# A fused attention-like product and mixture layer on one core: the first stage's opening in pairs of row tiles, and the last product by halves

## The chip, the cores and the metric

The kernel runs as one program on one core of a Trainium2 chip. The metric is the device time of one execution in microseconds (us). A core has five engines with an instruction queue each: TensorE (PE in the profile, with its weight loads as PEld), VectorE (DVE), ScalarE (ACT), GpSimd (POOL) and SyncE (SP), which here only starts transfers. Each engine takes its instructions in the order in which they stand, and waits on semaphores where another engine has to be done first. Data lie in an on-chip memory of 128 partitions; matrix products land in PSUM, eight banks of 128x512 float32.

## The reference

```python
x = x + xattn(layernorm(x), ctx, s1, z1, s2, z2)     # x: (2, 1024, 2048), ctx: (2, 2048, 2048)
x = x + ffn(layernorm(x), W_base, b_base, W_router, lora_A, lora_B)

def fake_quant(x, s, z): q = clip(round(x / s + z), 0, 255); return (q - z) * s
def xattn(x1, x2, ...): return matmul(fake_quant(x1, s1, z1), fake_quant(x2, s2, z2))
def ffn(x, ...):                                       # 8 experts of rank 16, the best 2 of each token
    w = top-2 softmax weights of x @ W_router.T
    h = einsum('td,erd->ter', x, lora_A)
    return x @ W_base.T + b_base + 2.0 * einsum('ter,eor,te->to', h, lora_B, w)
```

So there are two large products for each of two batches of 1024 tokens: the quantised rows with the quantised context, 2048x2048, and then the normalised result with W_base, 2048x2048. The second is done in three float16 products (high and low parts) to keep its precision.

## The kernel before, in words

**First stage (0 to 303 us).** For each batch b the 1024 tokens are eight row tiles T of 128 tokens. A row tile of x is loaded (`load_rows`, 1 MB), VectorE takes its statistics in four `bn_stats` of 512 elements and a `bn_aggr` (`ln_stats_of`), ScalarE takes a root (`ln_std_of`), VectorE turns it into scale and shift by six operations on 128x1 (`ln_scale_of`), ScalarE writes the quantised bytes (`ln_bytes_of`, tile q1u), TensorE turns them in eight transposes (`turn`, into PSUM bank 6), and ScalarE copies them out as float16 (`ln_copy`, tile q1T). The context comes in 32 slices n of 128 output columns (16 for each batch), 1 MB each: `load_ctx`, then bytes on ScalarE (`ctx_bytes_of`), then float16 on VectorE (`ctx_ready_of`). The product of slice n is made in three chunks (n, c) of 342 token columns, 16 matmuls each (`chunk`): chunk 0 needs row tiles 0 to 2, chunk 1 tiles 0 to 5, chunk 2 all eight. The chunks go round four PSUM banks. VectorE takes each chunk out and adds x (`take_y`); after chunk 2 ScalarE adds a column (`col_add_of`), writes the high half for the second stage (`hi_of`) and squares (`sq_of`); VectorE writes the low half (`lo_of`) and sums the squares (`acc_of`).

The order is written out by hand, engine by engine. The first three slices are interleaved in a group, as `ORDER` (line 44) says; from slice 3 on a loop takes one slice after the other. The tiles of batch 1 are worked in between: tiles 8 and 9 in the opening, the others at the slices in `LN_AT`. The waits that matter here: `turn(T)` waits for the bytes of T and for the copy of T - 1, since all share bank 6; a chunk waits for its context slice, its row tiles, and for the take of the chunk four places ahead of it; `take_y` waits for xT's slice in memory too.

**The parameters.** s1, z1, s2, z2 are single numbers. Four transfers spread each of them to a column of 128 partitions (line 627). VectorE derives 21 more columns of `par` from them. SP waits for these four transfers behind the load of row tile 0, ahead of row tile 1.

**Second stage (303 to 345 us)** makes row sums, the router's logits and the low-rank parts. **Third stage (345 to 1027 us)** is the product with W_base. Batch 0 comes in 32 plain tiles of 128x512, 48 matmuls each. Batch 1 is done in eight units i of seven half-depth products p of 24 matmuls each (`multiply`), from which VectorE puts four output quarters q together by seven additions (`take`). A quarter's end (`out_of`) is five operations on 128x512: two that need no product (mean and shift, L1292 and L1294), then scale and add the low-rank part (L1296), times the row scale (L1298), plus bias (L1301). The low-rank part is three matmuls (`quarter_lora`) which ScalarE takes out (`lora_of`). Then SP stores the quarter, 256 KB.

## Time and profile before

| | us |
|---|---|
| median of 3 runs | 1029.69 (1028.73 to 1030.63) |
| the profiled execution | 1028.86 |
| its span, from the first to the last instruction recorded | 1027.1 |
| TensorE busy in the span | 967.9 (94%) |
| VectorE busy | 798.7 (78%) |
| ScalarE busy | 470.3 (46%) |
| granted TensorE clock, mean (1 is full) | 0.988 |

The profile's page gives sums and the chain of waits that ended last. The trace behind it is asked for windows (busy time of each engine in a stretch), for the timeline of an engine (equal neighbours merged) and for the transfers. Busy time of matmuls is not TensorE at its peak: a 342 column chunk takes longer when the granted clock is at its lower level.

### The profile page before, as it was taken

To read this page: it belongs to the slowest core of one execution; us is meant where nothing else is said; L and a number is where in the kernel's file an instruction comes from. 1 tells how busy PE (TensorE), PEld (TensorE's weight loads), DVE (VectorE), ACT (ScalarE), POOL (GpSimd) and SP (SyncE) were. 2 spreads that over 40 slices of the span, in tenths; PEclk is the share of its full clock that TensorE was granted. 3 is DMA by queue.
4 is the path that set the end of the run, shared out by engine and by line. 5 is a ranking of instruction groups with operands and counts; after the bars stand their busy time and mean duration, and the time that the engine had idled before them with its cause. 6 is when DMAs were issued, how large, how long until landed. Compare 5 with 4: busy or idle time off the path is not lost.

```text
span 1027.1 us, 15016 instructions
## 1 busy us (share of the span) xinstructions
PE 967.9 (94%) x5847; PEld 523.5 (51%) x5847; DVE 798.7 (78%) x1503; ACT 470.3 (46%) x492; POOL 18.7 (2%) x40
## 2 busy tenths in 40 slices
PE   0478999999999999999999999999999999999997
PEld 0355666666679844444444444444444444444443
DVE  6767899788763787896788687775788798798775
ACT  4769989688652245543454433312223223322300
POOL 0000000000000000000000000000000000000000
PEclk9989999999999999999999999999999999999999
DMA  7836777587734236886566665238643243233220
GB/s 301 338 119 226 256 277 291 205 292 302 274 129 138 91 132 186 238 263 206 184 204 180 182 236 196 67 103 291 221 149 113 78 149 112 78 134 102 83 72 31
DMA packets 62590, 185.64 MB, mean 181 GB/s; under 512 B 7432, under 2 KB 19768, under 8 KB 56248
## 3 DMA queue, kind: packets, MB, share of 16 engines
q1 hardware_dynamic: 58360, 174.18, 48.3%
q10 hardware_dynamic: 2880, 8.39, 2.1%
q0 software_dynamic: 1280, 2.12, 2.0%
q8 instruction: 46, 0.75, 0.3%
q14 instruction: 24, 0.20, 0.1%
HBM read 151.07 MB, written 33.60 MB: 180 GB/s over the span
## 4 chain that ended last, share of the span: by engine, by line
PE 74%; DVE 4%; DMA 2%; ACT 1%; issue 1%; DVEq 0%; ACTq 0%
PE pair L1638 30%; PE pair L1661 28%; PE pair L1501 10%; PE pair L1617 4%; DMA w_r<-in_w_n 1%; PE pair L1607 1%; DMA spread<-scratch 1%; DMA scratch<-w_max 1%; DVE w_p L1123 0%; ACT w_r L730 0%; ACT xt L665 0%; ACT ctx_u L659 0%; PE pair L1583 0%; PE pair L1516 0%; PE pair L1509 0%
## 5 line engine op out<-in xcount | busy, mean ns | idle before, releaser
L1638 PE MATMUL pair<-x2p,w_p 128*128 128x512 f16 x1536 | 336.7, 379 | 1.0 <-DVE w_p L1123 1.0
L1638 PEld LDWEIGHTS pair<-x2p,w_p 128*128 128x128 f16 x1536 | 150.2, 98 | 181.9 <-DVE w_p L1123 1.5
L1501 PE MATMUL pair<-q1T,ctx_q 128*128 128x342 f16 x1536 | 234.0, 314 | 4.7 <-DVE xt L926 4.7
L1501 PEld LDWEIGHTS pair<-q1T,ctx_q 128*128 128x128 f16 x1536 | 150.1, 99 | 83.2 <-issue 6.3
L1661 PE MATMUL pair<-x2p,w_slot 128*128 128x512 f16 x768 | 169.2, 379 | 0.0
L757 ACT ACTIVATE sq<-pair,lsc 128x512 f32<-128x512 f32 x64 | 43.6, 682 | 226.0 <-PE pair L1617 192.3
L1661 PEld LDWEIGHTS pair<-x2p,w_slot 128*128 128x128 f16 x768 | 75.1, 98 | 90.7
L785 ACT ACTIVATE w_slot<-w_q,usc 128x1024 f16<-128x1024 f32 x32 | 36.5, 1146 | 95.7 <-DVE usc L1331 27.2
L1661 PE MATMUL pair<-x2p,x2p 128*128 128x512 f16 x336 | 74.3, 379 | 0.0
L659 ACT ACTIVATE ctx_u<-ctx_f,par 128x2048 uint8<-128x2048 f32 x32 | 66.6, 2081 | 1.6 <-DVE ctx_q L911 1.4
L926 DVE SCALAR_TENSOR_TENSOR xt<-pair,par,xt 128x342 f32<-128x342 f32 (+1 forms) x96 | 54.4, 567 | 15.6 <-PE pair L1501 15.6
L785 ACT ACTIVATE x2p<-w_q,usc 128x1024 f16<-128x1024 f32 x24 | 27.4, 1146 | 69.7 <-DVE usc L1331 15.5
L1355 DVE SCALAR_TENSOR_TENSOR w_slot<-w_q,usc,w_slot 128x1024 f16<-128x1024 f32 x32 | 40.6, 1282 | 22.8 <-ACT w_slot L785 22.8
L932 DVE SCALAR_TENSOR_TENSOR x2p<-xt,xs,x2p 128x1024 f16<-128x1024 f32 x32 | 41.0, 1283 | 18.6 <-ACT x2p L673 18.5
L665 ACT ACTIVATE xt<-xt,colt 128x1024 f32<-128x1024 f32 x32 | 36.6, 1144 | 38.3 <-DVE xt L926 38.3
L1481 PE MATMUL pair<-ident,q1w 128*128 128x128 f16 x128 | 12.2, 252 | 44.4 <-ACT q1u L642 23.5
L1661 PEld LDWEIGHTS pair<-x2p,x2p 128*128 128x128 f16 x336 | 32.9, 98 | 39.6
L1661 PE MATMUL pair<-x2p 128*128 128x512 f16 x240 | 52.9, 379 | 0.0
L1617 PE MATMUL pair<-hwT,b_p 128*128 128x512 f16 x192 | 51.9, 379 | 0.0
L1301 DVE SCALAR_TENSOR_TENSOR u<-sq,bias_s,u 128x512 f32<-128x512 f32 x64 | 48.1, 752 | 2.2
L1607 PE MATMUL pair<-ar_p,x2p 128*128 128x137 f16 x768 | 48.6, 224 | 0.0
L1607 PEld LDWEIGHTS pair<-ar_p,x2p 128*128 128x128 f16 x768 | 48.3, 98 | 0.1
(200 smaller groups left out, 1061.1 us busy)
## 6 DMA issues: line engine op xcount, KB each, us to landing
ctx_f<-in_ctx SPq DMA_DIRECT2D x32, 1024.0 KB, 7.0
rows<-in_x SPq DMA_DIRECT2D x16, 1024.0 KB, 8.8
xt<-in_xT SPq DMA_DIRECT2D x32, 512.0 KB, 4.4
w_r<-in_w_n SPq DMA_DIRECT2D x32, 512.0 KB, 7.4
w_f<-in_w_t SPq DMA_DIRECT2D x32, 512.0 KB, 5.6
...
```

What stands on the lines that cost most here:

```text
L659: A.activation(ctx_u[:, :], ctx_f[n % 2][:, :], ACT.Identity, bias=Z2, scale=IS2).then_inc(ctx_bytes, 1)
L757: A.activation(sq[m % 2][:, :], lora_bank(m)[:, :], ACT.Copy, scale=by).then_inc(lora_taken, 1)
L785: A.activation(w_of(i, p, 0), w_q[s][:, :, :], ACT.Copy, scale=usc[:, i % 2, (3 if by == 4 else 2):(4 if by == 4 else 3)]).then_inc(s_hi, 1)
L926: V.scalar_tensor_tensor(xt[n % 3][:, t], bank[at % RING][:, 0:WIDTH[c]], S12, xt[n % 3][:, t], ALU.mult, ALU.add).then_inc(y_taken, 1)
L932: V.scalar_tensor_tensor(x2p[b][:, j, 1, :], xt[n % 3][:, :], xs[:, b, 0:1], x2p[b][:, j, 0, :], ALU.mult, ALU.subtract).then_inc(lo_done, 1)
L1301: V.scalar_tensor_tensor(o[:, :], s[:, :], bias_s[:, j:j + 1], o[:, :], ALU.add, ALU.add).then_inc(u_ready, 1)
L1355: V.scalar_tensor_tensor(w_of(i, p, 1), w_q[s][:, :, :], usc[:, i % 2, (3 if by == 4 else 2):(4 if by == 4 else 3)], w_of(i, p, 0), ALU.mu ...
L1501: ins = M.matmul(bank[at % RING][:, 0:W3], ctx_q[n % NQ][:, k, :], q1T[b][:, k, c * W3:(c + 1) * W3], start=(k == 0), stop=(k == KT - 1))
L1607: ins = M.matmul(h_tile(b, t), x2p[b][:, k, xh, t * P:(t + 1) * P], ar_p[ah][:, k, :], start=(k == 0 and q == 0), stop=(k == KT - 1 and q ...
L1617: ins = M.matmul(lora_bank(m)[:, :], b_p[s][bh][:, :], hwT[b][hh][:, t], start=(q == 0), stop=(q == 2))
L1638: M.matmul(base_bank(m)[:, :], w_p[j % 2][wh][:, k, :], x2p[0][:, k, xh, t], start=(k == 0 and q == 0), stop=(k == KT - 1 and q == 2))
L1661: ins = M.matmul(product_bank(i, p)[:, :], w_of(i, p, wh)[:, k // 4, (k % 4) * P:(k % 4 + 1) * P], x_of(p, k, xh), start=(k == 0 and q == ...
```

## The change

1. **Parameters.** Each of the four numbers lands as one element on partition 0 (in a free corner of tile `acc`). VectorE widens them there to four rows of 128, TensorE turns each row into a column of PSUM bank 0, and VectorE copies the four columns to `par`. SP doesn't wait for the parameters any more.
2. **Row tile 0** is loaded in two halves; VectorE takes the first two `bn_stats` while TensorE turns the parameters.
3. **Row tiles in pairs.** `LN_GROUPS` sets groups of one or two tiles. `ln_stats_of` is done tile by tile, but mean, variance, root and the seven operations of `ln_scale_of` are done once for a group, on 128x2.
4. **Order.** The first nine chunks go (0,0) (1,0) (2,0) (0,1) (1,1) (2,1) (0,2) (1,2) (2,2). TensorE has chunk (0,0) already behind turn 2. ScalarE, VectorE and SP have new orders in the opening, and the tiles of batch 1 new places later.
5. **Ends of quarters.** The two operations that need no product (`out_base`) now stand ahead of the additions.
6. **Last unit.** TensorE does the last low-rank part ahead of product 5, and the last product in two halves of 256 columns in two banks. VectorE prepares the last quarter while TensorE works, and at the end has two operations on 128x256 for each half. Each half is stored by itself, 128 KB.

The core of the diff:

```diff
-ORDER = [(0, 0), (1, 0), (0, 1), (2, 0), (1, 1), (2, 1), (0, 2), (1, 2), (2, 2)]
+ORDER = [(n, c) for c in range(NCH) for n in range(3)]
-LN_AT = [2, 4, 7, 9, 11, 13]
+LN_GROUPS = [(0, 1), (1, 2), (3, 2), (5, 2), (7, 1), (8, 2), (10, 2), (12, 2), (14, 2)]
+STATS_AT = {2: 10, 3: 11, 6: 12, 7: 13, 10: 14, 11: 15}
+BYTES_AT = {3: 10, 4: 11, 7: 12, 8: 13, 11: 14, 12: 15}
...
             load_rows(0)
-            sp.wait_ge(par_landed, 16 * 4)
             load_rows(1)
             load_rows(2)
             load_ctx(0)
...
             load_rows(5)
             load_rows(6)
+            load_ctx(2)
+            load_rows(7)
             load_xt(0)
-            load_rows(7)
             load_xt(1)
+            load_ctx(3)
             load_xt(2)
+            load_rows(TT)
+            load_rows(TT + 1)
             sp.dma_start(bias_s[:, :], bias).then_inc(par_landed, 16)
-            load_ctx(2)
-            load_rows(TT)
-            load_ctx(3)
-            load_rows(TT + 1)
...
-                act.dma_start(par[:, i:i + 1], src.rearrange("(a b) -> a b", a=1).to_broadcast([P, 1])).then_inc(par_landed, 16)
+                act.dma_start(acc[0:1, 4 * P + i:4 * P + i + 1], src.rearrange("(a b) -> a b", a=1)).then_inc(par_landed, 16)
...
+            ln_bytes_of(1)
+            ln_bytes_of(2)
+            ln_copy(1)
+            ctx_bytes_of(1)
+            ln_std_of(2)
+            ln_copy(2)
+            ln_bytes_of(3)
+            ln_bytes_of(4)
+            ln_copy(3)
+            ln_std_of(3)
+            ctx_bytes_of(2)
+            ln_copy(4)
+            ln_bytes_of(5)
+            ln_std_of(4)
+            ln_bytes_of(6)
+            ln_copy(5)
+            ln_bytes_of(7)
+            ln_copy(6)
...
             dve.wait_ge(par_landed, 16 * 4)
+            V.tensor_copy(acc[0:1, 0:4 * P].rearrange("p (a b) -> p a b", a=4),
+                          acc[0:1, 4 * P:4 * P + 4].unsqueeze(2).to_broadcast([1, 4, P])).then_inc(par_wide, 1)
+            dve.wait_ge(half_landed, 16)
+            for q in range(2):
+                V.bn_stats(stats[0][:, q, :], rows[0][0][:, q * 512:(q + 1) * 512])
+            dve.wait_ge(par_turned, 1)
+            V.tensor_copy(par[:, 0:4], bank[0][:, 0:4]).then_inc(par_copied, 1)
...
+            ctx_ready_of(0)
+            ln_stats_of(3)
+            ln_stats_of(4)
+            ln_scale_of(2)
+            ctx_ready_of(1)
+            ln_stats_of(5)
+            ln_stats_of(6)
+            take_y(0, 0)
+            take_y(1, 0)
+            ln_scale_of(3)
+            ctx_ready_of(2)
+            ln_stats_of(7)
+            ln_scale_of(4)
             bound(0)
+            take_y(2, 0)
...
+            for i in range(4):
+                ins = M.transpose(bank[0][:, i:i + 1], acc[0:1, i * P:(i + 1) * P], identF[0:1, 0:1])
+            ins.then_inc(par_turned, 1)
...
+            def multiply_last():
+                i, p = UNITS - 1, PRODUCTS - 1
...
+                for h in range(2):
+                    for k in range(HALF):
+                        for q, (wh, xh) in enumerate(((0, 0), (0, 1), (1, 0))):
+                            ins = M.matmul(bank[LAST_BANK[h]][:, LAST[h]], w_of(i, p, wh)[:, k // 4, (k % 4) * P:(k % 4 + 1) * P], x_of(p, k, xh)[:, LAST[h]],
+                                           start=(k == 0 and q == 0), stop=(k == HALF - 1 and q == 2))
+                    ins.then_inc(last_half[h], 1)
...
+                for h in range(2):
+                    t = slice(c * CH + LAST[h].start, c * CH + LAST[h].stop)
+                    dve.wait_ge(last_half[h], 1)
+                    V.scalar_tensor_tensor(s[:, LAST[h]], bank[LAST_BANK[h]][:, LAST[h]], by, rstdB[:, t], ALU.mult, ALU.mult).then_inc(last_step, 1)
+                    dve.wait_ge(last_step, h + 4)
+                    V.tensor_tensor(o[:, LAST[h]], o[:, LAST[h]], s[:, LAST[h]], ALU.add).then_inc(last_ready[h], 1)
```

How the instructions stand on three places that the prediction speaks of. First TensorE at the program's start; q1w are a row tile's bytes, ctx_q a context slice, L1481 and L1582 are `turn`, L1489 and L1590 the row sums, L1501 and L1602 a chunk. Before:

```order
L1481 MATMUL pair3<-ident16_136,q1w0_0_66 128x128 x8
L1481 MATMUL pair3<-ident16_136,q1w0_1_67 128x128 x8
L1489 MATMUL pair3<-ones16_138,q1T0_51 128x1 x16
L1481 MATMUL pair3<-ident16_136,q1w0_0_66 128x128 x8
L1489 MATMUL pair3<-ones16_138,q1T0_51 128x1 x16
L1481 MATMUL pair3<-ident16_136,q1w0_1_67 128x128 x8
L1489 MATMUL pair3<-ones16_138,q1T0_51 128x1 x16
L1501 MATMUL pair0<-q1T0_51,ctx_q0_74 128x342 x16
```

And now:

```order
L1570 MATMUL pair0<-identF_137,acc_80 128x1 x4
L1582 MATMUL pair3<-ident16_136,q1w0_0_66 128x128 x8
L1582 MATMUL pair3<-ident16_136,q1w0_1_67 128x128 x8
L1590 MATMUL pair3<-ones16_138,q1T0_51 128x1 x16
L1582 MATMUL pair3<-ident16_136,q1w0_0_66 128x128 x8
L1590 MATMUL pair3<-ones16_138,q1T0_51 128x1 x16
L1602 MATMUL pair0<-q1T0_51,ctx_q0_74 128x342 x16
L1582 MATMUL pair3<-ident16_136,q1w0_1_67 128x128 x8
L1590 MATMUL pair3<-ones16_138,q1T0_51 128x1 x16
L1602 MATMUL pair0<-q1T0_51,ctx_q1_75 128x342 x16
```

The first chunk stood behind turn 3 and stands behind turn 2; the second follows turn 3, where it followed turn 5.

VectorE around the statistics of row tiles 6 and 7 (rows0_6_59 is tile 6, rows0_0_53 there tile 7; xt0_77 and xt1_78 are slices 0 and 1, taken by `take_y`). Before:

```order
L854 BN_STATS stats0_140<-rows0_6_59 128x6 x4
L859 MEMSET lnt_146 128x1
L860 BN_AGGR mv0_142<-stats0_140 128x2
L862 COPY mean1_144<-mv0_142 128x1
L863 TENSOR_SCALAR lnt_146<-mv0_142 128x1
L926 SCALAR_TENSOR_TENSOR xt0_77<-pair0,par_147,xt0_77 128x342
L869 RECIPROCAL lnt_146<-std1_145 128x1
```

And now, from tile 5 on:

```order
L892 BN_STATS stats1_141<-rows0_5_58 128x6 x4
L895 BN_AGGR mv1_143<-stats1_141 128x2
L892 BN_STATS stats0_140<-rows0_6_59 128x6 x4
L895 BN_AGGR mv1_143<-stats0_140 128x2
L901 COPY mean1_144<-mv1_143 128x2
L902 TENSOR_SCALAR lnt1_147<-mv1_143 128x2
L968 SCALAR_TENSOR_TENSOR xt0_77<-pair0,par_148,xt0_77 128x342
L968 SCALAR_TENSOR_TENSOR xt1_78<-pair0,par_148,xt1_78 128x342
L909 RECIPROCAL lnt1_147<-std1_145 128x2
```

The takes of the first two chunks now stand together, ahead of the scales of tiles 5 and 6.

VectorE at the program's end (u3_123 is the last quarter's output, p = 6's product lies in pair1). Before:

```order
L1384 TENSOR_TENSOR ct_135<-u3_134,pair1 128x512
L1292 SCALAR_TENSOR_TENSOR u3_123<-meanB_108,wsum_162,u3_123 128x512
L1294 TENSOR_TENSOR u3_123<-u3_123,shiftB_109 128x512
L1296 SCALAR_TENSOR_TENSOR sq1_125<-ct_135,usc_165,sq1_125 128x512
L1298 TENSOR_TENSOR sq1_125<-sq1_125,rstdB_107 128x512
L1301 SCALAR_TENSOR_TENSOR u3_123<-sq1_125,bias_s_157,u3_123 128x512
```

And now:

```order
L1448 TENSOR_TENSOR ct_135<-u2_133,pair3 128x512
L1359 SCALAR_TENSOR_TENSOR sq0_124<-ct_135,usc_166,sq0_124 128x512
L1361 TENSOR_TENSOR sq0_124<-sq0_124,rstdB_107 128x512
L1364 SCALAR_TENSOR_TENSOR u2_122<-sq0_124,bias_s_158,u2_122 128x512
L1489 SCALAR_TENSOR_TENSOR sq1_125<-pair1,usc_166,rstdB_107 128x256
L1491 TENSOR_TENSOR u3_123<-u3_123,sq1_125 128x256
L1489 SCALAR_TENSOR_TENSOR sq1_125<-pair1,usc_166,rstdB_107 128x256
L1491 TENSOR_TENSOR u3_123<-u3_123,sq1_125 128x256
```

Behind the last product stood six operations on 128x512; behind its second half now stand two on 128x256. The first four rows are product 5's.

## Rows read from the trace of the kernel before

**Rows 1.** Windows: stretch, busy (count) of PE, PEld, DVE, ACT, POOL, granted clock, transfers.
```profile
50.00:55.00 5.00, 3.65 (x15) 1.77 (x13) 1.20 (x5) 0.02 (x1) 0.00 (x0) 0.69 0.59 210
...
90.00:100.00 10.00, 6.58 (x34) 3.74 (x33) 9.69 (x22) 9.93 (x9) 0.00 (x0) 0.83 0.87 313
100.00:150.00 50.00, 49.49 (x395) 33.40 (x392) 44.53 (x88) 46.00 (x36) 0.00 (x0) 1.00 0.73 268
...
600.00:1000.00 400.00, 400.00 (x1855) 181.37 (x1854) 322.78 (x490) 111.20 (x129) 3.27 (x6) 1.00 0.39 133
```

**Rows 2.** Timeline of TensorE in the opening: start, length, instruction, idle before it.
```profile
37.37 3.47 PE L1501 MATMUL pair<-q1T,ctx_q 128*128 128x342 f16 x16
...
49.37 4.29 PE L1501 MATMUL pair<-q1T,ctx_q 128*128 128x342 f16 x16
...
59.60 1.01 PE L1481 MATMUL pair<-ident,q1w 128*128 128x128 f16 x8 [5.95 <-ACT q1T L650]
...
75.47 9.46 PE L1501 MATMUL pair<-q1T,ctx_q 128*128 128x342 f16 x64
...
93.84 6.48 PE L1501 MATMUL pair<-q1T,ctx_q 128*128 128x342 f16 x32 [3.42 <-DVE xt L926]
```

**Rows 3.** Timeline of VectorE in the opening.
```profile
6.61 2.47 DVE L854 BATCH_NORM_STATS2 stats<-rows 128x6 f32<-128x512 f32 x4 [5.50 <-DMA rows<-in_x]
...
10.59 0.16 DVE L869 RECIPROCAL lnt<-std 128x1 f32<-128x1 f32 x1
...
22.20 2.47 DVE L854 BATCH_NORM_STATS2 stats<-rows 128x6 f32<-128x512 f32 x4
...
25.11 0.15 DVE L862 COPY mean<-mv 128x1 f32<-128x1 f32 x1
...
26.45 1.28 DVE L911 TENSOR_SCALAR ctx_q<-ctx_u,par 128x2048 f16<-128x2048 uint8 x1
...
53.69 0.57 DVE L926 SCALAR_TENSOR_TENSOR xt<-pair,par,xt 128x342 f32<-128x342 f32 x1 [6.70 <-PE pair L1501]
...
93.12 0.57 DVE L926 SCALAR_TENSOR_TENSOR xt<-pair,par,xt 128x342 f32<-128x342 f32 x1
```

**Rows 4.** Timeline of ScalarE in the opening.
```profile
11.99 2.10 ACT L642 ACTIVATE q1u<-rows,lnt 128x2048 uint8<-128x2048 f32 x1 [2.13 <-DVE lnt L878]
...
18.12 2.08 ACT L659 ACTIVATE ctx_u<-ctx_f,par 128x2048 uint8<-128x2048 f32 x1
...
28.56 1.95 ACT L650 ACTIVATE q1T<-pair,par 128x2048 f16<-128x2048 uint8 x1
...
55.51 2.10 ACT L642 ACTIVATE q1u<-rows,lnt 128x2048 uint8<-128x2048 f32 x1 [5.49 <-DVE lnt L878]
...
77.22 1.13 ACT L665 ACTIVATE xt<-xt,colt 128x1024 f32<-128x1024 f32 x1
...
84.22 1.14 ACT L665 ACTIVATE xt<-xt,colt 128x1024 f32<-128x1024 f32 x1
```

**Rows 5.** Transfers by line: count, KB each, median us from issue to landing.
```profile
scratch<-w_max POOLq DMA_DIRECT2D x16, 1.0 KB, 3.4
par<-in_s ACTq DMA_DIRECT2D x2, 0.5 KB, 5.8
```

**Rows 6.** SyncE's queue: what it waited for, in all, times, longest.
```profile
SPq L400 <- DMA par<-in_z: 7.1, 1, 7.1
```

**Rows 7.** Timeline of TensorE at the end.
```profile
1014.56 5.34 PE L1661 MATMUL pair<-x2p,w_slot 128*128 128x512 f16 x24
```

**Rows 8.** Timeline of VectorE at the end.
```profile
1019.94 0.69 DVE L1384 TENSOR_TENSOR ct<-u,pair 128x512 f32<-128x512 f32 x1 [1.45 <-PE pair L1661]
...
1023.57 0.75 DVE L1301 SCALAR_TENSOR_TENSOR u<-sq,bias_s,u 128x512 f32<-128x512 f32 x1
```

**Rows 9.** Chain of waits: start and length of 96 matmuls of 137 columns.
```profile
348.65 5.99 PE pair L1607 x96
```

**Rows 10.** The page's group of weight loads for these matmuls.
```profile
L1607 PEld LDWEIGHTS pair<-ar_p,x2p 128*128 128x128 f16 x768 | 48.3, 98 | 0.1
```

More of the change, by code:

```diff
@@ L318, in xattn_ffn @@
         product = sem("product")
+        last_half = [sem(f"last_half{h}") for h in range(2)]
+        last_step = sem("last_step")
+        last_ready = [sem(f"last_ready{h}") for h in range(2)]
         p1_copied = sem("p1_copied")
@@ L384, in xattn_ffn @@
         OUTS = PLAIN + 4 * UNITS
+        LAST = [slice(h * CH // 2, (h + 1) * CH // 2) for h in range(2)]
+        LAST_BANK = [2, 3]
         def kept(n):
@@ L850, in ln_stats_of @@
                 b, s = T // TT, T % 2
+                g, m = LN_OF[T]
+                t0, w = LN_GROUPS[g]
                 row = rows[b][T % ROW_SLOTS[b]]
[L852 to L857 removed]
@@ new lines, in ln_stats_of @@
+                if T:
+                    dve.wait_ge(rows_landed[b][T % ROW_SLOTS[b]], 16 * ((T % TT) // ROW_SLOTS[b] + 1))
+                    for q in range(4):
+                        ins = V.bn_stats(stats[s][:, q, :], row[:, q * 512:(q + 1) * 512])
+                    ins.then_inc(ln_stat, 1)
+                dve.wait_ge(ln_stat, 2 * T + 1)
+                V.bn_aggr(mv[g % 2][:, m, :], stats[s][:, :, :].rearrange("p a m -> p (a m)")).then_inc(ln_stat, 1)
+                if m < w - 1:
+                    return
@@ L955, in _ @@
             V.tensor_scalar(C2, Z2, ROUND, ROUND, ALU.add, ALU.subtract).then_inc(par_step, 1)
+            dve.wait_ge(rows_landed[0][0], 16)
+            for q in range(2, 4):
+                ins = V.bn_stats(stats[0][:, q, :], rows[0][0][:, q * 512:(q + 1) * 512])
+            ins.then_inc(ln_stat, 1)
+            ln_stats_of(0)
             dve.wait_ge(par_step, 1)
```

285 lines of the change are left out of this document (163 added, 122 removed).

## The prediction

> **What bounds the kernel now.** I read the windows first. From 600 to 1000 us TensorE is busy all the time at a granted clock of 1.00, and from 100 to 150 us for 49.49 of 50 [rows 1]. Nothing that the change does to VectorE or ScalarE there can shorten it. The time to be had lies where TensorE stands: ahead of about 100 us, and behind its last matmul. So I read three timelines of the opening, and two of the end.
>
> In the opening TensorE has done two chunks by 53.7 us, at 37.37 and at 49.37, and stands again until 59.60; it is continuous only from there, with one more wait of 3.42 us, ended at 93.84 by a take of VectorE [rows 2]. The longest wait on VectorE is 6.70 us, until 53.69: it stands at the take of chunk (1,0), which stands on TensorE behind turns 4 and 5, and the scale of row tile 6 is queued behind that take [rows 3]. ScalarE waits 5.49 us for this scale, until 55.51 [rows 4], and TensorE for ScalarE's copy. A ring of three engines, closed by the order. Ahead of it each row tile costs VectorE 4.25 us (22.20 to 26.45), and ScalarE 2.0 for bytes and 1.85 for the copy (neighbouring starts lie that far apart).
>
> **The end.** TensorE's last product is 24 matmuls in 5.34 us from 1014.56, to 1019.90 [rows 7]. VectorE then does six operations, 1019.94 to 1024.32 [rows 8], 4.38 us, and the store follows. Of the six, the change leaves two behind the second half, on 256 columns. A 512 wide SCALAR_TENSOR_TENSOR takes 0.75 [rows 8], a 342 wide one 0.57 [rows 3], 1.06 ns a column, so 256 columns are 0.48; with the step between dependent operations two of them take 1.0 us. The 48 half matmuls: 342 columns take 145 ns each (9.46 for 64, less the last one's tail) [rows 2], 0.42 ns a column, so 256 take 109, and 48 take 5.24, where 24 wide ones take 5.18: +0.06. Their weight loads are doubled. Do they fit? 96 matmuls of 137 columns, each with its own load, take 5.99 us, 62 ns each [rows 9], though a load is shown with 98 ns [rows 10]; so loads lie beside matmuls and 109 ns is far above what they need.
>
> The Trainium skill ("TensorE: Matmul & The Clock Gate", Part 3, "The mechanism") says that a weight load overlaps with matmuls in flight only when it goes to other rows of the array; these take all rows. By that rule each half matmul would cost its load as well. The 62 ns of [rows 9] contradict it here.
>
> Is VectorE free at the second half's end? By the new order: the additions for product 4 at 1008.3 and 1009.0, quarter 1's end (three operations, 2.2) to 1011.8, the last quarter's preparation (two, and with the low-rank part three more, 3.7) to 1015.5, product 5 from there to 1016.2, quarter 2's end to 1018.4, the first half (ready 1017.2) to 1019.4. The second is ready at 1019.96 and done at 1021.0. That is 0.5 us of slack, and 3.3 us less than 1024.32. The store of 128 KB for 256 saves 0.2 by my choice, between 0 and half of what remains of the span (2.8, so 1.4). **End: -3.5**, from -2.5 (VectorE has no slack) to -4.7.
>
> The operations moved ahead of the additions in the other units are the same count. They put off a take by 1.4 us, while TensorE shows no wait at all from 600 to 1000 us [rows 1]; cost nothing, cover VectorE's 77 idle us there. If it were gone, 1.4 us in each of the eight units.
>
> **The parameters.** They land 5.8 us from issue [rows 5], the last issued at 2.2, so at 8.0; SP waits 7.1 for them [rows 6], and with it row tile 1. Now SP goes on at once: transfers run some 6 us earlier, and no row tile is waited for any more. One element's landing isn't in the trace. From below, near nothing: it could be 1 us. From above 5.8, if the many small pieces are not what costs. The nearest small transfer is the 1 KB at 3.4 [rows 5]; I take that, so landed 5.6. Then VectorE widens (0.7, as a 512 wide operation), takes two of four statistics (to 7.6) while TensorE turns, copies the columns and derives the first (to 8.2), takes the other two and the rest. Row tile 0's statistics ended at 9.1 and end at about 9.5; seven chained operations take 1.5 for 1.4 (10.59 to 11.99) [rows 3, 4]. So row tile 0's bytes start at 11.9, as before at 11.99. The spreading wins nothing by itself; what it wins is that tile 1 is there, and VectorE is at it 1.1 us earlier.
>
> The Trainium skill ("DMA: Bandwidth & Descriptors", "Latency and other measured facts") puts the least round trip of a tiny transfer near 0.8 us. Landed at 3.0 by that, the opening would win 2.6 us more; it is no term of the sum.
>
> **Pairs.** A tile's statistics are 2.9 us (22.20 to 25.11). A pair is 2 x 2.9 + 0.15 + 0.3 for the root on ScalarE + 1.3 for seven operations = 7.55, for 2 x 4.25 = 8.5 before: 0.95 less for a pair. The root is now waited for.
>
> **The order**, worked through (V VectorE, A ScalarE, P TensorE), a context's bytes 2.0 on A and 1.2 on V [rows 3, 4], a turn 1.0, a chunk 3.5 as the one at 37.37 while TensorE comes out of pauses, and 2.33 in a run [rows 2]:
> - V: tiles 1, 2 and their scale to 19.6, the other parameters (1.75) and context 0 to 22.5; tiles 3, 4, scale, context 1 to 31.3; tiles 5, 6 to 37.2; take (0,0).
> - A: bytes 0, context 0; copy 0 to 20.0; bytes 1, 2, copy 1, context 1 to 27.9; copy 2 to 30.5; bytes 3, 4 to 34.5; copy 3, once turn 3 is done, to 37.0.
> - P: chunk (0,0) 30.6 to 34.1, turn 3, chunk (1,0) to 39.0. V waits 1.3 for it and then takes it to 39.6: this is what is left of the 6.70. Scale of 5 and 6 to 40.9, context 2 to 42.1; chunk (2,0) to 45.7.
> - A: copy 4 to 41.9, bytes 5; V tile 7 to 45.2; A bytes 6, copy 5 to 49.3, bytes 7, P turn 6, chunk (0,1) to 54.4; A copy 6, context 3, copy 7 to 57.3.
> - P: chunks (1,1), (2,1), (0,2) to 63.5, with V behind each. Chunk (0,2) ended before at 75.0; it is the first step that needs all eight tiles.
> - From V's take of it (64.3; 76.3 before) ScalarE works slices 0 and 1. The step between their columns is 84.22 - 77.22 = 7.0 [rows 4], now 9.05, as the bytes of tile 9 stand between. So VectorE's take of (3,0), which follows ScalarE's squares, comes 18.3 us behind, where it came 16.4 behind (93.69) [rows 3]. TensorE starts (4,1) at **82.6 for 93.84**, after standing 2.9 us for 3.42.
>
> From there on the work left is the same on all engines: tile 9's bytes are done earlier, tile 10's later. TensorE sets the pace (49.49 of 50 busy), so the distance stays to the end of the stage. That is -11.2 by a sum without any slack in its hand-overs; some 20 of them lie on the path, at 0.05 each not counted: **opening -10.2**. Its bounds: parameters at 5.8 from issue (+2.4), and the lower clock level: a chunk takes 4.29 instead of 3.5 at 49.37 [rows 2], where the windows show 0.69 [rows 1], on four chunks +3; so from -5 to -14 (chunks at 2.33 from the start, and parameters early).
>
> **Sum.** 1028.86 (the profiled execution, span 1027.1) - 10.2 - 3.5 = 1015.2. It ran 0.8 below the median, 0.1 above the lowest; I add 0.3: **1015.5**.
>
> **Rivals.**
> 1. *The opening gives back about half.* Late parameters and chunks at the lower level, +5.4: 1020.9. For it: the chunks now come singly between pauses, and before, it was behind pauses that the clock fell (0.69, and 0.83 from 90 to 100 us) [rows 1]. Against: tile 0 isn't all of the opening. 0.15.
> 2. *ScalarE is the bound up to 190 us*, and what the opening wins is stood out there. For it: 46.00 of 50 busy [rows 1], a slice with tile bytes and copy needs 9 us of it for TensorE's 7. Then only the end is left: 1028.86 + 0.3 - 3.5 = 1025.7. Against: slices with a tile are half of them, and before it also idled 4 us in that window. 0.07.
> 3. *More*: TensorE warm early, parameters early: 1011. For it: chunks in a run are 2.33. 0.12.
> 4. *Slower.* The granted clock stays at its lower level through all fourteen chunks of the opening, since they are spread over 50 us. A chunk then takes 4.56 (342 columns at 1.2 GHz): four at +1.1 and ten at +2.2, 26 us, less the stall of 2.9 that this hides: 1015.5 + 23.5 = 1039. It decides from about eight of the ten running chunks at that level. Against: at 93.84 two chunks in a run took 6.48 for 4.7, so the level came back within them [rows 2]. 0.02.
> 5. *The half matmuls pay their loads*: 48 x 98 ns = +4.7, and the end is +1.4 instead of -3.5: 1020.2. For it: the page's rule. Against: [rows 9, 10]. 0.03.
>
> The forecast has 0.61. The range that leaves out 2 in 10 is 1010.5 to 1021. A measurement of this kernel tells 0.2% (2 us) from nothing; faster by more than that: 0.96, within it 0.02, slower 0.02.
>
> **What would show it.** In the changed profile: chunk (0,0) near 31 us, VectorE's wait at the take of (1,0) under 2 us for 6.70, chunk (4,1) near 83; the first stage's last matmul near 292 for 303; the third stage's length unchanged from first plain tile to last product; two 256 wide operations behind the last matmul, some 1 us. Wrong would be: row tile 0's bytes later than 13 us, new waits of TensorE between 100 and 290 us, half matmuls above 115 ns, or a VectorE that is still at quarter 2 when the second half is ready.

## The result, and the profile after

The changed kernel takes 1019.04 us (median of 4 runs, 1018.03 to 1020.31) for 1029.21 of the kernel before beside it (1027.64 to 1030.63). The ratio is 0.9902 [0.9883, 0.9922]. The forecast was 1015.5 with a range of 1010.5 to 1021: the sign and the range hold, and of the forecast gain of 14.2 us there came 10.2.

| | before | after |
|---|---|---|
| the profiled execution, us | 1028.86 | 1018.03 |
| its span | 1027.1 | 1016.3 |
| TensorE busy | 967.9 | 967.9 |
| VectorE busy | 798.7 | 791.0 |
| ScalarE busy | 470.3 | 469.3 |
| chunk (0,0) starts | 37.37 | 30.26 |
| chunk (4,1) starts | 93.84 | 82.80 |
| chunk (5,0) starts | 101.01 | 87.47 |
| last chunk of the first stage ends | 303.00 | 295.94 |
| last product starts | 1014.56 | 1007.50 |
| span's end behind that | 12.5 | 8.8 |

The table locates the 10.8 us between the two profiles. The opening wins 11.0 at chunk (4,1) and 13.5 at chunk (5,0). Of the 13.5, 0.85 is no gain: TensorE's row sums of tile 9 and turn of tile 10 stood ahead of (5,0) before, from 100.16 to 101.01, and stand behind it now, from 96.64. By the end of the first stage 7.06 are left. From there to the last product both kernels take 711.56 us. That they agree to the hundredth is chance: in the experiments below it is 710.1 to 713.4. The end wins the other 3.7.

First the opening. This is TensorE's timeline of the changed kernel (start, length, instruction, idle time before it and what ended it), as [rows 2] were of before:

```profile
30.26 3.76 PE L1602 MATMUL pair<-q1T,ctx_q 128*128 128x342 f16 x16 [3.03 <-ACT q1T L675]
...
34.71 2.48 PE L1602 MATMUL pair<-q1T,ctx_q 128*128 128x342 f16 x16
...
57.40 2.48 PE L1602 MATMUL pair<-q1T,ctx_q 128*128 128x342 f16 x16
64.78 1.03 PE L1582 MATMUL pair<-ident,q1w 128*128 128x128 f16 x8 [4.90 <-ACT q1u L667]
65.61 11.84 PE L1602 MATMUL pair<-q1T,ctx_q 128*128 128x342 f16 x64
...
78.13 11.83 PE L1602 MATMUL pair<-q1T,ctx_q 128*128 128x342 f16 x80
```

Chunk (0,2) is done at 59.88, where the forecast had 63.5. But then TensorE stands 4.90 us ahead of turn 8, a wait of which the prediction has nothing. The four chunks behind it take 11.84 us, where four behind one another took 9.46 in [rows 2]. The row at 78.13 is five chunks in a run: (4,1) is the third of them, and the wait of 3.42 us that stood ahead of it before [rows 2] is gone altogether.

The window behind the new wait (columns as in [rows 1]) shows the granted clock at 0.50, which is the lower of the two levels, 1.2 GHz:

```profile
65.00:70.00 5.00, 5.00 (x24) 2.98 (x23) 0.00 (x0) 4.97 (x5) 0.00 (x0) 0.50 0.60 213
```

Where does the 4.90 come from? Two timelines of the changed kernel tell it, first VectorE's and then ScalarE's:

```profile
37.23 0.57 DVE L968 SCALAR_TENSOR_TENSOR xt<-pair,par,xt 128x342 f32<-128x342 f32 x1 [0.22 <-PE pair L1602]
...
59.99 1.29 DVE L953 TENSOR_SCALAR ctx_q<-ctx_u,par 128x2048 f16<-128x2048 uint8 x1 [4.55 <-PE pair L1602]
61.20 0.16 DVE L909 RECIPROCAL lnt<-std 128x2 f32<-128x2 f32 x1
...
62.37 0.23 DVE L920 TENSOR_SCALAR lnt<-lnt,par 128x2 f32<-128x2 f32 x1
```

```profile
11.97 2.10 ACT L667 ACTIVATE q1u<-rows,lnt 128x2048 uint8<-128x2048 f32 x1 [1.51 <-DVE lnt L920]
...
62.63 2.10 ACT L667 ACTIVATE q1u<-rows,lnt 128x2048 uint8<-128x2048 f32 x1 [7.48 <-DVE lnt L920]
64.63 1.14 ACT L690 ACTIVATE xt<-xt,colt 128x1024 f32<-128x1024 f32 x1
```

The old ring is open: the wait of 6.70 us at the take of (1,0) [rows 3] is 0.22 now. But a ring of the same kind has closed further on. `ctx_q` has three buffers. VectorE's `ctx_ready_of(3)` writes over slice 0, so it waits until TensorE has done chunk (0,2), 4.55 us; the scale of row tiles 8 and 9 is queued behind it (61.20 to 62.60); ScalarE waits 7.48 us for that scale; and TensorE waits for the bytes.

How much of this lies on the way to chunk (4,1)? That chunk takes the bank of (3,0), so it needs VectorE's take of (3,0), which stands behind ScalarE's work on slices 0 and 1:

```profile
82.12 0.57 DVE L968 SCALAR_TENSOR_TENSOR xt<-pair,par,xt 128x342 f32<-128x342 f32 x1
```

The take ends at 82.69, and (4,1) starts at 82.80. ScalarE starts slice 0 at 64.63 (the last row of its timeline above), 18.1 us earlier, and that is 4.75 us behind the end of chunk (0,2): context slice 3 and the scale on VectorE and the bytes of tile 8 on ScalarE stand between. Turn 8 and the four slow chunks lie beside this chain. The experiments show it: wherever these orders are kept, (4,1) starts 22.9 us behind the end of (0,2), however long the four chunks take.

Then the middle of the stage, still TensorE, changed kernel:

```profile
91.33 2.48 PE L1602 MATMUL pair<-q1T,ctx_q 128*128 128x342 f16 x16 [1.37 <-DVE xt L968]
94.32 2.48 PE L1602 MATMUL pair<-q1T,ctx_q 128*128 128x342 f16 x16 [0.50 <-DVE xt L968]
...
105.17 0.55 PE L1590 MATMUL pair<-ones,q1T 128*128 128x1 f16 x16 [0.55 <-ACT q1T L675]
...
123.42 2.48 PE L1602 MATMUL pair<-q1T,ctx_q 128*128 128x342 f16 x16 [0.97 <-DVE xt L968]
126.40 2.48 PE L1602 MATMUL pair<-q1T,ctx_q 128*128 128x342 f16 x16 [0.50 <-DVE xt L968]
...
137.25 0.55 PE L1590 MATMUL pair<-ones,q1T 128*128 128x1 f16 x16 [0.55 <-ACT q1T L675]
...
189.37 6.48 PE L1602 MATMUL pair<-q1T,ctx_q 128*128 128x342 f16 x32
```

Three waits come back in the same form every 32.09 us (91.33, 123.42, and 155.50 follows), which is one round of four slices. With the last one, 0.83 at 187.56, the ten waits add up to 7.28 us. In the kernel before there were five, 2.51 us in all, behind chunk (5,0), and it ran without a stop for 14 and 18 us at a time:

```profile
100.56 0.61 PE L1481 MATMUL pair<-ident,q1w 128*128 128x128 f16 x8
101.01 14.11 PE L1501 MATMUL pair<-q1T,ctx_q 128*128 128x342 f16 x96
...
115.80 18.75 PE L1501 MATMUL pair<-q1T,ctx_q 128*128 128x342 f16 x128
134.75 1.47 PE L1501 MATMUL pair<-q1T,ctx_q 128*128 128x342 f16 x9 [0.21 <-DVE xt L926]
```

From (5,0) to the stage's end it is 208.47 us for 201.99, 6.5 more. 0.85 of it is the turn of tile 10 with the row sums of tile 9, which are only moved. 4.8 are waits. There are ten of them for five, and a chunk that ends in a stop takes 2.48 us where one in a run takes 2.33, which is another 0.8. So 5.6 us are given back. What holds TensorE up there stands on ScalarE, here in the changed kernel:

```profile
101.18 2.08 ACT L667 ACTIVATE q1u<-rows,lnt 128x2048 uint8<-128x2048 f32 x1
103.16 1.95 ACT L675 ACTIVATE q1T<-pair,par 128x2048 f16<-128x2048 uint8 x1
105.01 1.14 ACT L690 ACTIVATE xt<-xt,colt 128x1024 f32<-128x1024 f32 x1
```

In one slice it does the bytes of tile 11 and the copy of tile 10, 4 us together, beside the 5 us of the slice's own work. A slice is 7 us on TensorE. Both fall in one slice because `BYTES_AT` now has neighbours in it (3 and 4, 7 and 8, 11 and 12), and a tile's copy comes one slice behind its bytes. VectorE stands 3.81 us for ScalarE until 107.36, and then takes out late.

Last the end, VectorE of the changed kernel beside TensorE's last product, as [rows 7] and [rows 8] were of before:

```profile
1007.50 5.40 PE L1782 MATMUL pair<-x2p,w_slot 128*128 128x256 f16 x48
...
1011.28 0.48 DVE L1489 SCALAR_TENSOR_TENSOR sq<-pair,usc,rstdB 128x256 f32<-128x256 f32 x1
...
1011.80 0.42 DVE L1491 TENSOR_TENSOR u<-u,sq 128x256 f32<-128x256 f32 x1
...
1012.94 0.48 DVE L1489 SCALAR_TENSOR_TENSOR sq<-pair,usc,rstdB 128x256 f32<-128x256 f32 x1 [0.72 <-PE pair L1782]
1013.46 0.42 DVE L1491 TENSOR_TENSOR u<-u,sq 128x256 f32<-128x256 f32 x1
```

48 half matmuls take 5.40, 0.06 more than the 24 wide ones. VectorE waits 0.72 us for the second half and is done 0.98 behind TensorE's end, where it was 4.42 before.

### The profile page after: what moved, and what is told of

The parts are those of the page before. It is cut to its first block, busy times and chain, and to the rows that moved or that the text cites. A ratio compares the mean times of both kernels' runs of the same rounds, so it can differ in the third digit from the quotient of the medians.

```text
span 1016.3 us, 15003 instructions
## 1 busy us (share of the span) xinstructions
PE 967.9 (95%) x5875; PEld 524.7 (52%) x5875; DVE 791.0 (78%) x1445; ACT 469.3 (46%) x485; POOL 18.8 (2%) x40
## 4 chain that ended last, share of the span: by engine, by line
PE 75%; DVE 4%; DMA 3%; ACT 0%; issue 0%; DVEq 0%
PE pair L1747 31%; PE pair L1770 28%; PE pair L1602 10%; PE pair L1726 4%; DMA w_r<-in_w_n 1%; PE pair L1716 1%; DMA spread<-scratch 1%; DMA scratch<-w_max 1%; PE pair L1782 1%; DVE w_p L1180 0%; ACT w_r L765 0%; DVE acc L987 0%; PE pair L1692 0%; PE pair L1617 0%; PE pair L1610 0%
## 5 line engine op out<-in xcount | busy, mean ns | idle before, releaser
L1602 PE MATMUL pair<-q1T,ctx_q 128*128 128x342 f16 x1536 | 233.6, 313 | 10.2 <-DVE xt L968 4.8
L1602 PEld LDWEIGHTS pair<-q1T,ctx_q 128*128 128x128 f16 x1536 | 149.7, 98 | 88.9 <-issue 10.4
L1770 PE MATMUL pair<-x2p,w_slot 128*128 128x512 f16 x744 | 163.8, 379 | 0.0
L1770 PEld LDWEIGHTS pair<-x2p,w_slot 128*128 128x128 f16 x744 | 72.7, 98 | 87.8
L776 ACT ACTIVATE w_p<-w_f,wsc 128x1024 f16<-128x1024 f32 x32 | 34.9, 1139 | 28.8 <-DVE wsc L1165 28.8
```

Of the source, the lines that this page charges most:

```text
L1602: ins = M.matmul(bank[at % RING][:, 0:W3], ctx_q[n % NQ][:, k, :], q1T[b][:, k, c * W3:(c + 1) * W3], start=(k == 0), stop=(k == KT - 1))
L1770: ins = M.matmul(product_bank(i, p)[:, :], w_of(i, p, wh)[:, k // 4, (k % 4) * P:(k % 4 + 1) * P], x_of(p, k, xh), start=(k == 0 and q == ...
```

## The experiments

Each was timed in three rounds with the kernel before on the same chip; the ratio is to that, and 0.001 of it is 1.0 us. Where two kernels differ by less than their runs spread, the step that was changed is read in the trace. "Stage end" is the end of the last chunk of the first stage: 303.00 before, 295.94 in the changed kernel. Experiments are edits of the changed kernel, unless it is said otherwise.

How much does one trace scatter? The first experiment (bytes in every other slice) and the one with the old end leave everything up to chunk (4,1) as it is in the changed kernel. Chunk (0,2) ends at 59.88 in the changed kernel and at 61.33 and 62.11 in these two, and (4,1) starts at 82.80, 84.28 and 85.05. The scatter of 2.2 us arises ahead of the end of (0,2), where chunk (0,0) takes 3.76, 4.54 and 4.72. The distance from there to (4,1) is 22.92, 22.95 and 22.94, so it is the better yardstick for the opening. There is a second such place. This is TensorE with the old end:

```profile
59.63 2.48 PE L1603 MATMUL pair<-q1T,ctx_q 128*128 128x342 f16 x16
...
85.05 7.13 PE L1603 MATMUL pair<-q1T,ctx_q 128*128 128x342 f16 x48 [1.16 <-DVE xt L964]
...
191.54 4.81 PE L1603 MATMUL pair<-q1T,ctx_q 128*128 128x342 f16 x32
```

The last row's two chunks take 4.81 us. In the changed kernel they take 6.48 (the row at 189.37), with the same orders and the same wait of 0.8 ahead. From 190 to 195 us the granted clock is 0.67 there (first row) and 1.00 with the old end (second row):

```profile
190.00:195.00 5.00, 5.00 (x25) 2.88 (x24) 1.44 (x3) 0.64 (x1) 0.00 (x0) 0.67 0.36 139
190.00:195.00 5.00, 5.00 (x40) 3.85 (x40) 2.30 (x10) 0.15 (x1) 0.00 (x0) 1.00 0.74 262
```

So 1.7 us at a stage's end can be this clock alone. The kernel before, the scale ahead, the mended opening and the spread parameters without SP's wait have the long form, the others the short one.

**The tiles' bytes in every other slice.**

```diff
-BYTES_AT = {3: 10, 4: 11, 7: 12, 8: 13, 11: 14, 12: 15}
+BYTES_AT = {3: 10, 5: 11, 7: 12, 9: 13, 11: 14, 13: 15}
```

> The changed kernel won 13.6 us up to chunk 16 of the first stage (87.5 us for 101.0 before), but only 7.1 us up to the stage's end. This run moves one thing: the bytes and copies of batch 1's row tiles on ScalarE (and their turns on TensorE) stand at slices 3, 5, 7, 9, 11, 13, where the changed kernel has them at 3, 4, 7, 8, 11, 12; the statistics stay in pairs and where they are. Theory A (two tiles' ScalarE work in neighbouring slices, 23.3 us for TensorE's 21, is what makes VectorE late and TensorE wait): the waits of TensorE fall from some 2.5 us in every 12 chunks to about 1.0 as before, twelve chunks take 30.6 for 32.1 us, the stage ends near 291.5 for 295.9 and the whole is 3 to 5 us shorter than the changed kernel, so near 1014.5. Theory B (it is VectorE's two statistics in neighbouring slices and the scale that stands ahead of a take): nothing changes, 12 chunks stay at 32, the whole stays within 1 us of the changed kernel (1019).

1016.79 us, ratio 0.9872 [0.9855, 0.9888]; stage end 290.79. Behind chunk (5,0) the waits are 1.36, 0.50, 0.35, 0.36 and 0.63, in all 3.20 for 7.28, and six chunks run without a stop:

```profile
95.75 2.48 PE L1602 MATMUL pair<-q1T,ctx_q 128*128 128x342 f16 x16 [0.50 <-DVE xt L968]
...
98.92 14.11 PE L1602 MATMUL pair<-q1T,ctx_q 128*128 128x342 f16 x96
...
125.84 2.48 PE L1602 MATMUL pair<-q1T,ctx_q 128*128 128x342 f16 x16 [0.35 <-DVE xt L968]
```

A round of four slices takes 30.09 us (95.75 to 125.84) for 32.09, and VectorE's wait for ScalarE near 107 us falls from 3.81 to 1.82. From chunk (5,0), at 88.92, the rest of the stage takes 201.87 us for 208.47. Of these 6.6 us, 1.7 are the clock behind 190 us: the kernel with the old end, which has the changed kernel's spacing and no such dip, takes 206.72. So these six numbers are worth 4.9 of the 5.6 us. That the kernel before takes nearly the same, 201.99, is in part chance: it has the slow form of the two chunks, and one turn less. ScalarE's work is the same; only its spacing is other: in 100 to 150 us it is busy for 48.37, and TensorE for 49.65, where the changed kernel has 45.87 and 47.44. Not all of it reaches the end: of 5.2 us at the stage's end 3.6 are left at the last product, for TensorE waits 2.43 us for `w_p` at 390.10 in place of 0.98.

**The tiles of batch 1 each by itself**, with the numbers of the kernel before.

```diff
-LN_GROUPS = [..., (10, 2), (12, 2), (14, 2)]
+LN_GROUPS = [...] + [(T, 1) for T in range(10, 16)]
-STATS_AT = {2: 10, 3: 11, 6: 12, 7: 13, 10: 14, 11: 15}
-BYTES_AT = {3: 10, 4: 11, 7: 12, 8: 13, 11: 14, 12: 15}
+STATS_AT = {2: 10, 4: 11, 7: 12, 9: 13, 11: 14, 13: 15}
+BYTES_AT = {2: 10, 4: 11, 7: 12, 9: 13, 11: 14, 13: 15}
...
```

`SCALE_AT` and `LOAD_AT` follow the new groups.

> As the changed kernel, but from row tile 10 on each tile is a group of its own, with statistics, scale and bytes at the slices of the kernel before (2, 4, 7, 9, 11, 13). Both theory A and B: twelve chunks take 30.6 us, as before, the stage ends near 291, the whole near 1014.5. If it doesn't (12 chunks still 32), the loss sits in something else that the change did to the stage, such as the later loads, and both theories fall. Tiles alone cost VectorE some 0.95 us a pair more, beside TensorE's work, so nothing.

1017.88 us, 0.9878 [0.9864, 0.9893]; stage end 293.78. The waits behind chunk (5,0) are 0.40 to 0.44, except for the last of 1.27, 3.31 in all. From (5,0), here at 92.48, the rest takes 201.30 us, with the turn of tile 10 ahead of it as before. So pairs aren't what costs in the middle, the neighbouring places are. The stage ends 3 us behind that of the first experiment. At (4,1), here at 86.29, 2.0 of them are there, and 1.6 of these are the scatter ahead of the end of (0,2), 62.92 for 61.33. The other 0.4 is the distance, 23.4 for 22.9, and tile 10's bytes stand one slice earlier there. The last 1.0 is mostly waits behind (4,1), 3.85 us for 3.20.

**The scale of tiles 8 and 9 ahead of the waiting `ctx_ready_of(3)`.**

```diff
+            ln_scale_of(5)
             take_y(1, 1)
             ctx_ready_of(3)
-            ln_scale_of(5)
```

> In the changed kernel VectorE stands 4.55 us at context slice 3, which must wait for chunk (0,2) since it takes slice 0's buffer; the scale of tiles 8 and 9 is behind it, ScalarE's bytes of tile 8 behind that, and turn 8 on TensorE: TensorE stands 4.90 us until 64.78, then its clock is at 0.50 and four chunks take 11.84 for 9.4 us. Here the scale stands ahead of the take of (1,1). Theory C (this wait is on the path): TensorE goes on at 60 and the stage ends 7 us earlier. Theory D (what sets the opening's end is when ScalarE starts slice 0, which hangs on VectorE's take of (0,2), not on turn 8): ScalarE starts slice 0 at 62.3 for 64.6, TensorE does the next chunks earlier and then stands some 4 us at the ring of four banks, chunk (4,1) starts at 80.4 for 82.8, and comes out of the stand at the lower clock: the whole gains 0 to 1.5 us.

1019.98 us, 0.9894 [0.9877, 0.9911]; stage end 296.16. Turn 8 no longer waits, and chunk (1,2) starts at 62.57 for 65.61. But two waits take its place:

```profile
62.57 9.46 PE L1602 MATMUL pair<-q1T,ctx_q 128*128 128x342 f16 x64
...
74.02 0.68 PE L1582 MATMUL pair<-ident,q1w 128*128 128x128 f16 x8 [1.44 <-ACT q1u L667]
74.49 6.47 PE L1602 MATMUL pair<-q1T,ctx_q 128*128 128x342 f16 x32
83.08 3.21 PE L1602 MATMUL pair<-q1T,ctx_q 128*128 128x342 f16 x21 [2.12 <-DVE xt L968]
```

Chunk (4,1) is at 83.08 for 82.80, but (0,2) ended at 62.28 here for 59.88. The distance between them is 20.8 us for 22.9. So the edit wins 2.1 us of chain, and not the 4.90 of the wait and the 2.4 of slow chunks: they lay beside ScalarE's slices, which start behind the take of (0,2), here at 64.86, and have tile 9's bytes between slice 0 and 1. The medians don't tell the two kernels apart.

**Both mended**: the scale ahead of `take_y(1, 1)`, `ctx_ready_of(3)` behind the take of (0,2), and tile 9's bytes ahead of slice 0.

```diff
             ln_bytes_of(TT)
+            ln_bytes_of(TT + 1)
...
-                if n == 0:
-                    ln_bytes_of(TT + 1)
...
             xscale(0)
-            take_y(1, 1)
-            ctx_ready_of(3)
             ln_scale_of(5)
+            take_y(1, 1)
             take_y(2, 1)
             take_y(0, 2)
+            ctx_ready_of(3)
```

> As scale_first, and context slice 3 on VectorE behind the take of (0,2), and the bytes of tile 9 on ScalarE ahead of slice 0, where ScalarE idles, as in the kernel before. Theory D: ScalarE starts slice 0 near 61.0, the take of (3,0) comes 16.1 us behind that for 18.1, chunk (4,1) starts at 77.5 for 82.8; the stage ends 4 to 5 us earlier, the whole is near 1014.5. Theory C: 7 us, no more than in scale_first. If the rest of the stage gives it back (theory E: from slice 4 on ScalarE and VectorE are the bound, not TensorE), the stage's end doesn't move by more than 1 us in either.

1016.08 us, 0.9863 [0.9848, 0.9878]; (4,1) at 79.65, where 77.5 was expected, and stage end 292.74, 3.2 us earlier. The distance from the end of (0,2) to (4,1) is 17.1 us, for 20.8 with the scale ahead alone and 22.9 in the changed kernel. With tile 9's bytes done in the idle time of ScalarE (7.48 us), the shorter distance from slice 0 to 1 pays. A wait of 1.83 us ahead of (4,1) is left.

**The mended opening and the bytes in every other slice.** The edits are those of the last and of the first experiment.

> opening_fixed and bytes_spread together. opening_fixed ended the first stage at 292.7 and bytes_spread at 290.8, for 295.9 of the changed kernel. If the two gains add (the one is the start of chunk (4,1), the other the waits in each group of 12 chunks behind it), the stage ends at 287.6 and the whole is near 1013. If they are one and the same slack (what the opening wins, ScalarE's bound takes back), it ends at 290.5 and the whole is near 1016.

1007.79 us (1006.80 to 1008.24), 0.9801 [0.9786, 0.9815]. The stage ends at 285.61, two us below the sum of the two gains. Most of this is scatter: the first experiment's trace reached (4,1) 1.5 us late. From (5,0) on it takes 202.1 us here, for 201.87 there, and the distance from (0,2) to (4,1) is 17.1, as with the mended opening. The waits behind (5,0) are 1.36, 0.49, 0.36, 0.35 and 0.64. This is the fastest version, though the runs of the next one overlap with it.

**The same, with tile 10's statistics behind the take of (3,0).**

```diff
-            ln_stats_of(STATS_AT[2])
...
+                if n == 3:
+                    ln_stats_of(STATS_AT[2])
```

> The fastest so far (1007.79 us: the opening's VectorE order mended, and the bytes of batch 1's tiles in every other slice) with one edit: the statistics of row tile 10 stand behind the take of (3,0) on VectorE instead of ahead of it. Theory A (the 1.83 us for which TensorE stands ahead of chunk (4,1), at 78.87, is VectorE's, which does 2.9 us of statistics ahead of the take that the chunk's bank waits for): the stall goes, (4,1) at 77 to 77.5, the stage ends at 283.8 to 284.5, the time is 1006 to 1006.8. Theory B (the take waits for ScalarE's squares, and the statistics lie in that wait): the stall stays within 0.3 us, and the statistics push VectorE's later takes; time 1007.5 to 1008.5.

1008.74 us, 0.9809 [0.9793, 0.9826]; stage end 286.35. Neither theory holds as it stands:

```profile
72.97 7.13 PE L1601 MATMUL pair<-q1T,ctx_q 128*128 128x342 f16 x48
81.89 4.81 PE L1601 MATMUL pair<-q1T,ctx_q 128*128 128x342 f16 x32 [1.79 <-DVE xt L967]
88.32 2.48 PE L1601 MATMUL pair<-q1T,ctx_q 128*128 128x342 f16 x16 [1.63 <-DVE xt L967]
```

The wait ahead of (4,1) is gone, and stands with 1.79 ahead of the next chunk. I read it so that VectorE has this work to do by about 82 us wherever it stands. The 0.7 us between the two stage ends is within the scatter.

**The end of the kernel before**: last unit, last product and last store as they were; the two operations ahead of the additions stay.

> The changed kernel with the last unit's end of the kernel before: one last product of 24 matmuls on 512 columns, six operations behind it, one store of 256 KB. The preparation ahead of the additions (out_base) stays, so four operations are left behind the product. Theory of the prediction: from TensorE's last matmul to VectorE's last operation 0.96 us in the changed kernel and 4.38 before; here four operations, 2.9 us, and the store 0.3 us more: 2.3 us slower than the changed kernel. The stage behind the opening is the same, so nothing else moves. Rival (the end was hidden by the store's landing or the halves cost TensorE): under 1 us of difference.

1021.59 us, 0.9934 [0.9919, 0.9949]; stage end 296.43. Four operations are behind the product:

```profile
1008.17 5.34 PE L1771 MATMUL pair<-x2p,w_slot 128*128 128x512 f16 x24
...
1013.55 0.69 DVE L1444 TENSOR_TENSOR ct<-u,pair 128x512 f32<-128x512 f32 x1 [1.45 <-PE pair L1771]
1014.27 0.75 DVE L1355 SCALAR_TENSOR_TENSOR sq<-ct,usc,sq 128x512 f32<-128x512 f32 x1
1015.06 0.69 DVE L1357 TENSOR_TENSOR sq<-sq,rstdB 128x512 f32<-128x512 f32 x1
1015.78 0.75 DVE L1360 SCALAR_TENSOR_TENSOR u<-sq,bias_s,u 128x512 f32<-128x512 f32 x1
```

From the product's start to the span's end it is 11.2 us, for 8.8 with the halves and 12.5 before. The end's 3.7 split into 1.3 for the two operations ahead of the additions, and 2.4 for the halves and the early preparation.

**The tiles of batch 0 each by itself** (`LN_GROUPS` with eight single tiles, and the roots and scales that belong to them).

> The changed kernel with row tiles 1 to 6 in groups of their own (the same order, each root and each scale twice on 128x1 instead of once on 128x2). By the prediction a pair saves VectorE 0.95 us, and by the changed kernel's trace 1.3 for the second scale and 0.3 for the second mean and variance: three pairs, so 3 to 4.5 us later at the take of (0,2), as VectorE is 90% busy there. Rival (the opening hangs on ScalarE's and TensorE's ring, VectorE has slack): under 1.5 us later at chunk (4,1).

1022.58 us, 0.9945 [0.9930, 0.9960]; (4,1) at 89.27; stage end 300.66. Three pairs and 0.95 us each, as the prediction has them, would be 3 us. The end of (0,2) is at 66.32, and the distance from there to (4,1) is 22.9 as with pairs, so all of the cost is ahead of it: 6.4 us against the changed kernel's trace, 4.2 against the one with the old end. That one has 4.72 us for chunk (0,0), as here, and between the stage ends it is 4.2 us too. So the pairs are worth about 4 us, and the rest is scatter.

**The parameters by four spread transfers again**, without the wait on SP.

```diff
-                act.dma_start(acc[0:1, 4 * P + i:4 * P + i + 1], src.rearrange("(a b) -> a b", a=1)).then_inc(par_landed, 16)
+                act.dma_start(par[:, i:i + 1], src.rearrange("(a b) -> a b", a=1).to_broadcast([P, 1])).then_inc(par_landed, 16)
```

> The changed kernel with the parameters spread by four transfers to 128 partitions, as before, and none of the change's widening, four transposes and copy; SP still does not wait for them. Of row tile 0's statistics two stand ahead of the wait for the parameters. By the prediction the spreading wins nothing by itself, what wins is that SP doesn't wait: row tile 0's bytes start at 11 to 12.5 us (the transfers take 5.8 from the last issue at 2.2, so 8.0, then 0.4, two statistics and 2.2 of small work), chunk 16 within 1 us of the changed kernel's 87.5, the whole within 1 us. Rival: the four times 128 small pieces are in the way of the row tiles' loads on the same 16 engines, now that these stream from the start: they land at 10 or later, all of the opening is 2 to 3 us later.

1023.57 us, 0.9957 [0.9940, 0.9974]; stage end 302.48. This is VectorE's row at the parameters:

```profile
13.40 0.16 DVE L997 RECIPROCAL par<-par 128x1 f32<-128x1 f32 x1 [5.35 <-DMA par<-in_z]
```

The last of the four is issued at about 2.2, so it lands after 11.2 us, for 5.8 before [rows 5]. Row tile 0's bytes start at 17.23, and chunk (0,0) at 35.51.

**The same, with SP's wait for them put back**, ahead of row tile 1.

```diff
             load_rows(0)
+            sp.wait_ge(par_landed, 16 * 4)
             load_rows(1)
```

> The changed kernel with the parameters spread by four transfers again, and with SP waiting for them behind row tile 0, as in the kernel before; the rest as changed. It stands beside the same kernel without SP's wait (1023.57 us, parameters landed at 13.40 us, ScalarE's first bytes at 17.23, chunk (4,1) later, first stage's end 302.48). Theory A (it is the row tiles streaming on the same engines that make the spread transfers late, 11.2 us instead of 5.8): with SP standing, the parameters land at 8.0 to 9.0 us, row tile 0's bytes start at 12.0 to 13.0, row tile 1 is there some 6 us later, and then VectorE waits for tile 1; chunk (0,0) starts at 31 to 34, the time is 1019 to 1023, not above that of the kernel without the wait. Theory B (the spread transfer takes 11 us with these neighbours whether or not SP stands): parameters at 13, and with SP's wait row tile 1 later still, the time 1026 or more.

1020.85 us, 0.9921 [0.9906, 0.9935]; stage end 298.56. Theory A holds. The parameters are there at 7.95, and VectorE waits only little for tile 1:

```profile
7.95 0.16 DVE L998 RECIPROCAL par<-par 128x1 f32<-128x1 f32 x1 [0.58 <-DMA par<-in_z]
...
12.67 2.47 DVE L893 BATCH_NORM_STATS2 stats<-rows 128x6 f32<-128x512 f32 x4 [0.68 <-DMA rows<-in_x]
```

Tile 0's bytes start at 11.77, earlier than in the changed kernel (11.97), and chunk (0,0) at 32.15 for 30.26. The old way to load the parameters, wait and all, costs 2.1 us of the stage against the kernel with the old end, and 2.6 against the changed kernel. Dropping the wait alone costs 3.9 more at the stage's end, 1.7 of it by the clock behind 190 us, and 2.3 at the end of chunk (0,2) (66.46 for 64.19); the medians differ by 2.7.

## Why the prediction was right, and where it was wrong

**The opening up to chunk (4,1): the number right, the way only in part.** 82.6 was forecast (plus 1 for hand-overs), 82.80 came. Tile 0's bytes at 11.9 came at 11.97, chunk (0,0) at 30.6 at 30.26, the take of (1,0) waits 0.22 for a forecast 1.3. Then two errors cancel. Chunk (0,2) ends at 59.88, not 63.5: ScalarE has the bytes of tile 6 at 43.44, since the root of tile 7 that stands ahead of them waits only for its input, and not, as I had it, for VectorE's tile 7 as a whole (45.2), and chunks behind others take 2.48 us, not the 3.5 that I took from [rows 2]. And the prediction's V line ends with chunk (0,2) and doesn't go through `ctx_ready_of(3)`, whose buffer comes free only then, nor through the scale behind it and tile 8's bytes behind that. It lets ScalarE start slice 0 0.8 us behind the end of (0,2), where it took 4.75. So slice 0 starts at 64.63 for 64.3. From there on the prediction's chain is right: 18.1 us to the end of the take of (3,0), for 18.3. (The 16.4 that it gives for the kernel before is counted from ScalarE's slice 0 at 77.22; from the take at 76.3 it is 17.4.) The stall of 2.9 us forecast ahead of (4,1) was not there, because TensorE had stood 4.90 us earlier and was slow for 2.4 more. The number owes something to luck as well: the same opening reached (4,1) at 84.28 and 85.05 in two other traces, so it wins 9 to 11 us, not 11.0 for certain.

**The step that failed** is "From there on the work left is the same on all engines... so the distance stays to the end of the stage". The work is the same, its spacing isn't. The prediction read TensorE's 49.49 of 50 as a property of the stage, when it was one of the places `LN_AT` gave to the tiles. The change put them in neighbouring slices, and of the 12.7 us won at chunk (5,0), the moved turn left out, 5.6 were given back: the stage's last matmul came at 295.94, not near 292. Rival 2 had the right engine, and the right rule ("a slice with tile bytes and copy needs 9 us of it for TensorE's 7"), but treated it as a question of ScalarE's sum. The runs show that the sum is not the bound: with the bytes in every other slice and the same sum of work, the waits fall from 7.28 us to 3.20. A wrong sign that the prediction named, "new waits of TensorE between 100 and 290", is what the profile has.

**How the shortfall adds up.** Forecast were -10.2 for the opening carried to the stage's end; measured are -7.06 there. The difference of 3.1 is 5.6 given back, less 2.5 on the credit side: 0.8 at (4,1) (11.0 for 10.2, the haircut of 1.0 was not needed in this trace), and 1.7 from there to (5,0), which the prediction did not count. That is the clock: two chunks took 6.48 us behind the stall [rows 2] and take 4.8 now.

**The end: right.** -3.5 forecast, -3.7 measured. Half matmuls at 109 ns: 48 of them take 5.40 with tail, 112 each, so rival 5 (loads paid for, 4.7 us) falls; [rows 9] were the better guide. (Rival 5's end should read +1.2, which is 4.7 less 3.5; its 1020.2 is right.) The rule that the prediction weighed against them, from the Trainium skill ("TensorE: Matmul & The Clock Gate", Part 3, "The mechanism"), does not hold for these half matmuls either. Two operations of 0.48 and 0.42 are done 0.98 behind the matmuls, for 1.0. VectorE's slack was 0.72 for a forecast 0.5.

**The middle at nothing: right.** TensorE is busy for 400.00 of 400 us from 600 to 1000 in the changed kernel too.

**The parameters: right, with a bound too small.** "The spreading wins nothing by itself; what it wins is that tile 1 is there": tile 0's bytes come at 11.97 with the elements and at 11.77 by the old way with SP's wait, so this holds. But the bound that I gave for late parameters, 5.8 us from issue and +2.4, was the landing of transfers that had only row tile 0 beside them. Beside row tiles 1 and 2 they take 11.2, and the stage ends 6.5 later. The elements land at 6.44 where the prediction had 5.6. They are not faster than spread transfers with SP standing: the columns stand in `par` at 8.14, for 7.95. They are what allows SP to go on.

**The pairs: size too small.** Forecast 0.95 each, about 3 for the three of batch 0; measured about 4 (4.2 against a trace with equally slow first chunks, 6.4 against the changed kernel's own). Which step costs the other 1 us is not shown.
